# Image keys of eight batches as four pairs with seven products instead of eight

## What is computed

```
q     = heads(x @ to_q_w)
h_txt = sdpa(q, heads(ctx[0:77]   @ to_k_w),        heads(ctx[0:77]   @ to_v_w))
h_obj = sdpa(q, heads(ctx[77:81]  @ to_k_object_w), heads(ctx[77:81]  @ to_v_object_w))
h_oth = sdpa(q, heads(ctx[81:85]  @ to_k_others_w), heads(ctx[81:85]  @ to_v_others_w))
h_ip  = sdpa(q, heads(ctx[85:512] @ to_k_ip_w),     heads(ctx[85:512] @ to_v_ip_w))
out   = merge(h_txt + h_obj + h_oth + h_ip) @ to_out_w + to_out_b + x
```

## Time and profile before

| | |
|---|---|
| median of three runs | 2381.95 us |
| the profiled execution | 2381.67 us, its span 2379.5 us |
| TensorE busy | 2365.9 us |
| VectorE busy | 1835.2 us |
| ScalarE busy | 1775.6 us |
| GpSimd busy | 412.5 us |
| image-key products, line 1661 | 1848 matmuls, 364.2 us |
| granted TensorE clock | 1.00 |
| moved by transfers | 370.12 MB, 156 GB/s in the mean |

### The profile page before, as it was taken

One profiled execution on the slowest core, in us unless ns is written; L12 is line 12 of the kernel. 1 busy time (PEld: TensorE's weight loads), 2 busy tenths in 40 slices (PEclk: granted clock), 3 DMA queues, 4 the chain that ended last, 5 costly groups with the idle time before them and its releaser, 6 DMA issues.

```text
span 2379.5 us, 37663 instructions
## 1 busy us (share of the span) xinstructions
PE 2365.9 (99%) x12801; PEld 1805.1 (76%) x12801; DVE 1835.2 (77%) x3291; ACT 1775.6 (75%) x3906; POOL 412.5 (17%) x564
## 2 busy tenths in 40 slices
PE   9999999999999999999999999999999999999999
PEld 8999999998999986566666666666666666666665
DVE  4457777732333489999999999999999999999994
ACT  4343433332223369999999999999999999999995
POOL 0000000000000023413223133133132231231310
PEclk9999999999999999999999999999999999999999
DMA  9445444374644555545555555555455555555542
GB/s 339 161 128 159 150 136 141 109 268 147 232 167 174 182 174 153 148 129 154 152 143 146 134 148 159 137 146 151 128 156 154 134 150 141 144 161 128 147 132 78
DMA packets 371749, 370.12 MB, mean 156 GB/s; under 512 B 110046, under 2 KB 298590, under 8 KB 371558
## 3 DMA queue, kind: packets, MB, share of 16 engines
q1 hardware_dynamic: 334384, 306.14, 46.7%
q10 hardware_dynamic: 37174, 61.59, 7.0%
HBM read 215.57 MB, written 83.89 MB: 126 GB/s over the span
## 4 chain that ended last, share of the span: by engine, by line
PE 97%; ACT 2%; issue 0%; DMA 0%; DVE 0%; ACTq 0%
PE st_ps L1661 17%; PE s_ps L489 13%; PE st_ps L509 12%; PE om_ps L523 12%; PE om_ps L544 11%; PE om_ps L567 11%; PE s_ps L1713 7%; PE om_ps L1713 4%; PE s_ps L1681 3%; PE st_ps L1713 3%; ACT s_ps L689 1%; PE om_ps L1730 1%; ACT probs L681 1%; PE om_ps L602 1%; PE st_ps L1621 0%
## 5 line engine op out<-in xcount | busy, mean ns | idle before, releaser
L689 ACT ACTIVATE s_ps<-s_ps,negmax 128x427 f32<-128x427 f32 x1280 | 767.8, 608 | 21.6 <-DVE small L759 21.6
L750 DVE TENSOR_REDUCE negmax<-s_ps 128x2 f32<-128x854 f32 x640 | 666.0, 1041 | 75.4 <-PE s_ps L489 69.1
L681 ACT ACTIVATE probs<-st_ps 128x1024 f32<-128x1024 f32 x632 | 656.1, 1038 | 15.2 <-PE st_ps L509 3.7
L489 PE MATMUL s_ps<-kpack,qpack 96*128 96x512 f32 x1280 | 420.9, 410 | 2.1 <-ACT s_ps L689 2.1
L509 PE MATMUL st_ps<-qpack,kpack 104*128 104x512 f32 x1264 | 405.4, 402 | 2.5 <-ACT probs L681 2.5
L447 POOL TENSOR_TENSOR small<-small,negmax 128x616 f32<-128x616 f32 x160 | 196.5, 1228 | 999.8 <-DVE negmax L767 999.6
L1661 PE MATMUL st_ps<-ctx_split,w_split_ip 128*128 128x428 f32 x1848 | 364.2, 358 | 0.0
L1661 PEld LDWEIGHTS st_ps<-ctx_split,w_split_ip 128*128 128x128 f32 x1848 | 347.4, 188 | 15.2 <-issue 1.0
L489 PEld LDWEIGHTS s_ps<-kpack,qpack 96*128 96x128 f32 x1280 | 223.4, 189 | 177.6 <-ACT s_ps L689 81.0
L544 PE MATMUL om_ps<-xs,wq 128*128 128x512 f32 x1200 | 340.6, 394 | 0.0
L567 PE MATMUL om_ps<-heads,wo 128*128 128x512 f32 x1125 | 320.8, 394 | 0.0
(11 more groups left out here) (116 smaller groups left out, 2437.8 us busy)
## 6 DMA issues: line engine op xcount, KB each, us to landing
qpack<-q_out SPq DMA_DIRECT2D x240, 256.0 KB, 4.7
kpack<-kT SPq DMA_DIRECT2D x240, 217.5 KB, 2.9
kT<-k_out ACTq DMA_DIRECT2D x154, 217.5 KB, 3.3
ctx_split_raw<-in_ctxT SPq DMA_DIRECT2D x128, 214.0 KB, 4.6
tok_pair<-in_ctxT SPq DMA_DIRECT2D x48, 512.0 KB, 4.7
xs_raw<-in_xT SPq DMA_DIRECT2D x85, 256.0 KB, 3.8
out<-in_xT SPq DMA_DIRECT2D x75, 256.0 KB, 4.0
out_yT<-out SPq DMA_DIRECT2D x75, 256.0 KB, 2.1
```

The source lines that it names most:

```text
L489: last = nc.tensor.matmul(s_ps[:, n % 2, z, :], qpack[r][0:ROWS_S, j, t * P:(t + 1) * P], kpack[r][0:ROWS_S, j, :], start=True, stop=True)
L681: nc.scalar.activation(probs[:, at:at + 2, :], transposed(u, duo), ACT.Exp).then_inc(p_done, 1)
L689: last = nc.scalar.activation(s_ps[:, n % 2, z, SMALL:TOK], s_ps[:, n % 2, z, SMALL:TOK], ACT.Exp, bias=negmax[:, r, IP, j, t:t + 1], accu ...
L750: nc.vector.tensor_reduce(negmax[:, r, IP, j, t0:t0 + 2], s_ps[:, n % 2, :, SMALL:TOK], AX_X, ALU.max, negate=True).then_inc(s_max, 1)
```

## The change

The batches 3 to 10 are taken in four pairs. In a pair, B11 and B21 are the two halves (512 channels each) of the first batch's context, B12 and B22 those of the second's; the weights of the output blocks 0 and 1 and of 2 and 3 form the other operand, in the same halves. T1 to T4 are sums of the context halves, S1 to S4 sums of the weight halves. Seven products of halves then give the eight that the four double blocks need, with additions at the end. The fifth block is made for each batch as before, in two halves.

A pair is 18 groups (`K_GROUPS`: number of the operand, kind of bank, half), each 4 chunks times three passes, 12 matmuls. The eight operands of a pair (`K_OPERANDS`: B11, T3, T2, T4, B21, T1, B22, B12) go through three slots (`K_SLOTS`), each split in one piece of 4 x 428 elements. VectorE makes the sums T (`key_sum`) and the additions (`add_group`); an addition stands ahead of the split of the same step. ScalarE copies the first product (`keep_x`) and ten blocks per pair (`keep_group`). The stores of a pair's blocks are issued by SP (`store_group`), which also loads the raw context of the pair after next behind the store of group 14 (`load_raw`). The weight sums S are loaded, summed and split in batch 2. The small products move up by one batch each, and the loads of `wq` and `x` move behind all pairs.

```diff
+K_PAIRS = ((3, 4), (5, 6), (7, 8), (9, 10))
+K_PAIRED = tuple(b for pair in K_PAIRS for b in pair)
+K_OPERANDS = (B11, T3, T2, T4, B21, T1, B22, "B12")
+K_SLOTS = 3
+K_GROUPS = ((0, "X", 0), (0, "X", 1), (0, "F", 0), (1, "Q", 0), (1, "Q", 1), (2, "U", 0), (2, "U", 1),
+            (3, "Q", 0), (3, "Q", 1), (4, "X", 0), (4, "X", 1), (4, "F", 0), (5, "U", 0), (5, "U", 1),
+            (6, "U", 0), (6, "U", 1), (6, "F", 1), (7, "F", 1))
+K_OUT = {7: (0, 2), 8: (0, 3), 9: (0, 0), 10: (0, 1), 11: (0, 4), 12: (1, 2), 13: (1, 3), 14: (1, 0), 15: (1, 1), 17: (1, 4)}
+K_OUT_ORDER = tuple(K_OUT.values())
+U_ADDS = 10
+S_PARTS = (S1, S2, S3, S4)
...
-        ORDER += [("k", run, m) for m in k_slots(run)]
-        ORDER += {TXT + 1: [("s", 2, 0)], TXT + 2: [("s", 3, 0)]}.get(run, [])
+        if run - TXT not in K_PAIRED:
+            ORDER += [("k", run, m) for m in k_slots(run)]
+        elif K_PAIRED.index(run - TXT) % 2 == 0:
+            ORDER += [("p", K_PAIRED.index(run - TXT) // 2, i) for i in range(len(K_GROUPS))]
+        ORDER += {TXT: [("s", 2, 0)], TXT + 1: [("s", 3, 0)]}.get(run, [])
...
+    SUMS[("k", before_pairs, 0)] = ("sw", 0)
+    for m, parts in ((1, (S3, S2)), (2, (S1, S4))):
+        SPLITS.setdefault(("k", before_pairs, m), []).extend(("sw", i, 0) for i in parts)
+    for pp in range(len(K_PAIRS)):
+        ahead = [("k", before_pairs, 3), ("k", before_pairs, 4)] if pp == 0 else [("p", pp - 1, 15), ("p", pp - 1, 17)]
+        for j, step in enumerate(ahead + [("p", pp, i) for i in (2 if pp else 0, 3, 6, 9, 11, 13)]):
+            SPLITS.setdefault(step, []).append(("z", pp, j))
+    T_SUMS = {}
+    for pp in range(len(K_PAIRS)):
+        ahead = [("k", before_pairs, 3), ("k", before_pairs, 4)] if pp == 0 else [("p", pp - 1, 16), ("p", pp, 0)]
+        for i, step in zip((T3, T2, T4, T1), ahead + [("p", pp, 3), ("p", pp, 7)]):
+            T_SUMS[step] = (i, pp)
...
+    def stage_done(engine, z):
+        pp, j = divmod(z, len(K_OPERANDS))
+        if j in (0, 1, 6):
+            engine.wait_ge(z_acc, 3 * pp + {0: 1, 1: 2, 6: 3}[j])
+        elif j == 2:
+            engine.wait_ge(u_acc, 4 * pp + 4)
+        else:
+            engine.wait_ge(k_acc, pair_base(pp) + {3: 2, 4: 5, 5: 7, 7: 10}[j])
...
+        def store_group(pp, i):
+            run, m = pair_block(pp, i)
+            k0 = k_num(run, m)
+            sp.wait_ge(k_lo, k0 + 1)
+            sp.wait_ge(k_fill, k0 - k_base(TXT) + 1)
+            for part in (HI, LO):
+                sp.dma_start(d["kT"][run - TXT, part, m * P:(m + 1) * P, N_TXT:TOK],
+                             k_out[:, k0 % KR, part, 0:SM + IPN - 1].bitcast(F32)).then_inc(k_stored[k0 % KR], 16)
+        def load_raw(pp):
+            if pp < 2:
+                sp.wait_ge(k_acc, k_base(before_pairs + pp))
+            else:
+                sp.wait_ge(piece_lo, split_upto(("z", pp - 2, len(K_OPERANDS) - 1)))
+            for h, k in ((0, 0), (1, 1), (1, 0), (0, 1)):
+                sp.dma_start(raw[pp % 2][:, h, k, :, :],
+                             d["ctxT"][K_PAIRS[pp][h], k * CC2 * P:(k + 1) * CC2 * P, TOK - IPN:TOK]
+                             .rearrange("(n p) t -> p n t", p=P)).then_inc(raw_in[pp % 2][h][k], 16)
...
+        for r in range(2):
+            sp.wait_ge(v_stored[r], 16 * len(range(r, v_all, 2)) + 32 * len(range(r, TILE_PAIRS, 2)))
+        load_s_quarters()
+        load_raw(0)
+        load_raw(1)
+        store_late_small()
+        for pp in range(len(K_PAIRS)):
+            for i in K_OUT:
+                store_group(pp, i)
+                if i == 14:
+                    if pp + 2 < len(K_PAIRS):
+                        load_raw(pp + 2)
+                    else:
+                        for n in range(CC):
+                            load_c(K_LOAD[behind_pairs + pp + 2 - len(K_PAIRS)], n)
+        for b in range(K_PAIRED[-1] + 2, BATCH - 1):
+            if TXT + b > behind_pairs + 1:
                 for n in range(CC):
-                    load_halves("v", 1, n)
-            if b == 4:
-                store_late_small()
-            if b == 5:
+                    load_c(K_LOAD[TXT + b], n)
...
+            elif kind == "z":
+                i, z = K_OPERANDS[n], z_number(which, n)
+                if z < K_SLOTS:
+                    act.wait_ge(s_acc, 4)
+                    act.wait_ge(sv_stored, 32)
+                else:
+                    stage_done(act, z - K_SLOTS)
+                if i in T_ORDER:
+                    act.wait_ge(t_raw, summed(i, which))
+                else:
+                    h, k = {B11: (0, 0), B21: (0, 1), B22: (1, 1), "B12": (1, 0)}[i]
+                    act.wait_ge(raw_in[which % 2][h][k], raw_landed(which))
+                nc.scalar.activation(slots[z % K_SLOTS][:, HI, :, :], z_raw(which, n), ACT.Copy).then_inc(piece_hi, 1)
...
+        def keep_x(pp, t):
+            act.wait_ge(u_acc, 4 * pp + t + 1)
+            if pp > 0:
+                act.wait_ge(u_add, U_ADDS * pp)
+            nc.scalar.activation(u2_k[:, t, :], bank(pp, "X", t), ACT.Copy).then_inc(x_sb, 1)
+        def keep_group(pp, i):
+            run, m = pair_block(pp, i)
+            k0, (to, at, n) = k_num(run, m), k_cols(run)
+            _, kind, t = K_GROUPS[i]
+            if kind in "QU":
+                act.wait_ge(u_add, U_ADDS * pp + {7: 5, 8: 6, 12: 7, 13: 8, 14: 9, 15: 10}[i])
+            else:
+                act.wait_ge(k_acc, k0 + 1)
+            act.wait_ge(k_stored[k0 % KR], stored_upto(k0 % KR, k0))
+            src = u3_k[:, t, :] if i in (12, 13) else bank(pp, kind, t)
+            nc.scalar.activation(k_out[:, k0 % KR, HI, to:to + n], src[:, at:at + n], ACT.Copy).then_inc(k_hi, 1)
...
+        def key_sum(i, pp):
+            b11, b21, b12, b22 = (raw[pp % 2][:, h, k, :, :] for h in range(2) for k in range(2))
+            if i == T3:
+                if pp == 0:
+                    dve.wait_ge(s_acc, 4)
+                    dve.wait_ge(sv_stored, 32)
+                else:
+                    dve.wait_ge(piece_lo, split_upto(("z", pp - 1, 1)))
+                dve.wait_ge(raw_in[pp % 2][1][1], raw_landed(pp))
+                dve.wait_ge(raw_in[pp % 2][1][0], raw_landed(pp))
+                to, a, b, op = t3_raw[:, :, :], b22, b12, ALU.subtract
+            elif i == T2:
+                if pp > 0:
+                    dve.wait_ge(piece_lo, split_upto(("z", pp - 1, 2)))
+                dve.wait_ge(t_raw, summed(T3, pp))
+                dve.wait_ge(raw_in[pp % 2][0][0], raw_landed(pp))
+                to, a, b, op = t2_raw[:, :, :], t3_raw[:, :, :], b11, ALU.add
+            elif i == T4:
+                stage_done(dve, z_number(pp, 3) - K_SLOTS)
+                dve.wait_ge(t_raw, summed(T2, pp))
+                dve.wait_ge(raw_in[pp % 2][0][1], raw_landed(pp))
+                to, a, b, op = z_raw(pp, 3), b21, t2_raw[:, :, :], ALU.subtract
+            else:
+                stage_done(dve, z_number(pp, 5) - K_SLOTS)
+                to, a, b, op = z_raw(pp, 5), b12, b11, ALU.subtract
+            nc.vector.tensor_tensor(to, a, b, op).then_inc(t_raw, 1)
...
+        def add_group(pp, i):
+            _, kind, t = K_GROUPS[i]
+            u2, u3, n = u2_k[:, t, :], u3_k[:, t, :], U_ADDS * pp
+            if i in (5, 6):
+                dve.wait_ge(u_acc, 4 * pp + t + 3)
+                dve.wait_ge(x_sb, 2 * pp + t + 1)
+                if pp > 0:
+                    dve.wait_ge(u_add, n)
+                    dve.wait_ge(k_lo, pair_base(pp) - 3)
+                nc.vector.tensor_tensor(u2, bank(pp, "U", t), u2, ALU.add).then_inc(u_add, 1)
+                dve.wait_ge(u_add, n + 2 * t + 1)
+                nc.vector.tensor_tensor(u3, bank(pp, "Q", t), u2, ALU.add).then_inc(u_add, 1)
+            elif i in (7, 8, 14, 15):
+                k0 = k_num(*pair_block(pp, i))
+                dve.wait_ge(k_acc, k0 + 1)
+                dve.wait_ge(u_add, n + (4 if i < 10 else 8))
+                nc.vector.tensor_tensor(bank(pp, kind, t), bank(pp, kind, t), u2, ALU.add).then_inc(u_add, 1)
+            elif i in (12, 13):
+                dve.wait_ge(k_acc, k_num(*pair_block(pp, i)) + 1)
+                dve.wait_ge(u_add, n + 4)
+                nc.vector.tensor_tensor(u3, bank(pp, kind, t), u3, ALU.add).then_inc(u_add, 1)
+        def keep_group(pp, i):
+            run, m = pair_block(pp, i)
+            k0, (to, at, n) = k_num(run, m), k_cols(run)
+            _, kind, t = K_GROUPS[i]
+            src = u3_k[:, t, :] if i in (12, 13) else bank(pp, kind, t)
+            dve.wait_ge(k_hi, k0 + 1)
+            nc.vector.tensor_tensor(k_out[:, k0 % KR, LO, to:to + n], src[:, at:at + n],
+                                    k_out[:, k0 % KR, HI, to:to + n].bitcast(F32), ALU.subtract).then_inc(k_lo, 1)
...
+            if kind == "p":
+                add_group(a, b)
+                if b - 1 in K_OUT:
+                    keep_group(a, b - 1)
+                if b == len(K_GROUPS) - 1:
```

(117 more changed lines are left out.)

54 lines of the change are left out of this document (46 added, 8 removed).

## The result

The changed kernel takes 2368.57 us in the median (2368.26 to 2369.55, four runs), the kernel before 2382.11 us (2381.77 to 2382.32, four runs) on the same chip: the ratio is 0.9942, with an interval of [0.993, 0.9954]. That is 13.5 us less; 2367.7 us were forecast. The profiled execution took 2368.36 us, span 2366.6.

A forecast was written before the change was run, and what follows sets the result against it. TensorE was taken as the bound, busy 2365.9 of 2379.5 us. 2381.7 - 18.7 (matmuls) + 4.6 (transitions) = 2367.6, against the median 2367.9; forecast 2367.7 us, 8-in-10 range 2362.5 to 2376.5.

The forecast's parts named there:

- What the change takes away: Key stage: a pair needs 216 matmuls where two batches cost 240, at 0.1952 us each; four pairs save 18.7 us.
- The four durations: Lengths taken from earlier trace rows for VectorE's long and short operations and ScalarE's splits and copies: 1.94, 0.60, 1.62, 0.53 us.
- L: A VectorE sum or lower split of 1712 elements: 1.94 us, ends 1.49 and 2.28.
- H: ScalarE's upper split of 1712 elements: 1.62 us, ends 1.26 and 1.90.
- The transition: Between two pairs: a 22.1 us VectorE and ScalarE chain makes TensorE wait 1.3 us before group 7; three times, 4.6 us lost.
- The first pair and the edges: The first pair's operands are made beside batch 2, batch 11's splits in groups 14 to 17; claimed loss 0.
- Transfers, 0: Moved loads arrive in time and stores on SP, at 4.2 us landing, keep no place of k_out waiting; claimed loss 0.
- Stores leave ScalarE: In the pairs' blocks, stores move off ScalarE, which loses 0.81 us of issuing per block, none on the path.
- No wait at all: Rival, at the transitions: the chain is 1.3 us shorter, so TensorE never waits; 2363.0 us, chance 0.12.
- VectorE as the bound: Rival, in the pairs: longer VectorE operations or a wrongly walked order of waits; between 2371 and 2377 us, chance 0.17.
- The ring: Rival: late stores on SP hold up k_out's four places, then ScalarE, VectorE and TensorE; slower than before, 2389 or 2409 us, chance 0.06.

## Why the prediction was right

- **What the change takes away.** 888 matmuls at line 1940 and 864 at line 1987 are the 1752 that were forecast; a pair without a wait lasts 42.18 us, where two batches took 46.8. Four times that is 18.5 us (forecast 18.7).
- **The four durations.** The rows of the trace after, by form, answer to the earlier trace rows (busy us, mean ns, idle ahead):

```profile
L1687 DVE TENSOR_TENSOR k_ops<-ctx_raw,k_ops 128x1712 fp32r<-128x1712 f32 x16 | 31.0, 1935 | 3.1 <-ACT k_ops L1484 3.1
...
L1484 ACT ACTIVATE k_ops<-t_raw 128x1712 fp32r<-128x1712 f32 x8 | 13.1, 1635 | 19.3 <-DVE t_raw L1727 18.3 <-POOL k_out L1875 1.0
...
L1759 DVE TENSOR_TENSOR om_ps<-om_ps,u_k 128x428 f32<-128x428 f32 x8 | 4.8, 605 | 2.1 <-PE om_ps L1987 2.1
```

  L was 1.94 in the prediction, H 1.62, the addition written back into PSUM 0.60 of 0.60 to 0.68: all three were right within 1%. The straight line between two sizes held.
- **The transition.** Forecast 22.1 us for the chain, 1.3 us of wait, 1.5 us with the weight load, three times 4.6 in all; measured 22.20, 1.28 to 1.30, 1.5 and 4.6. T2 was 0.7 us early for group 5, as forecast (621.76 against 622.48 us); T3 1.6 us early for group 3 (616.21 against 617.79), where 0.7 was forecast. The prediction's own durations give 1.4 there (10.3 us of chain, group 3 due 11.7 us after group 15); its 0.7 was a slip on which nothing else rests.
- **The first pair and the edges** cost nothing: PE's waits show none there.
- **Transfers, 0.** No copy of the pairs waited for a store. The stores of 568 to 742 us landed in 2.5 us (median), where 4.2 was taken. But SP's one queue does what was feared. Its timeline in the first pair's last groups:

```profile
608.25 2.53 SPq L1342 DMA_DIRECT2D ctx_raw<-in_ctxT  x4
610.88 4.32 SPq L1332 DMA_DIRECT2D kT<-k_out  x4
```

  The stores issued from 604 to 606.5 us, ahead of these loads, and the four from 609 to 616 us, behind them (count, KB each, median us to landing):

```profile
kT<-k_out SPq DMA_DIRECT2D x2, 217.5 KB, 2.1
...
kT<-k_out SPq DMA_DIRECT2D x4, 217.5 KB, 8.5
```

  A store behind the 3424 KB takes 8.5 us in the median (10.3 the first) instead of 2.1, and as its place is wanted only some 25 us later, nobody waits. That is what the Trainium skill's "DMA: Bandwidth & Descriptors" (Queues, rings and completion order) says of one ring worked off in order; the trace agrees. With three places one copy of the pairs waited for a store (1.6 us), and TensorE for none.
- **Where it was wrong: "Stores leave ScalarE, which loses 0.81 us of issuing per block, none of it on the path."** True of the kernel before, where that sentence came from, but not of the changed one: with the stores left on ScalarE the change gains nothing (2381.39 us). With this order of the sums the move is not a detail beside the change but a condition of it, and the forecast came out because it was made in the same diff. With T2 behind T3 it is no condition: there most of the gain is left with the stores on ScalarE (2371.4 us).
- **The rivals.** No wait at all (2363.0) is what the version with T2 moved comes to, 2364.11. VectorE as the bound: with 130 us of work in 173 it wasn't. The ring: not in the pairs.
- **What stays open.** The last key block starts 13.94 us earlier (872.29 and 858.35 us), near the 14.1 forecast; the end of the span only 12.9. From that block's start to the end there are 1507.21 us in the trace of before, 1508.25 after, and between 1507.4 and 1508.3 in the experiments. So up to 1 us is lost in attention, as large as the spread between these traces; no run here tells what it is.

## What to carry to other kernels

When TensorE is the bound, work moved onto half-idle engines is free only if their order is: walk the list of each in-order engine through the one place where operands are made one behind another, with durations taken from rows of nearby sizes, and compare its length with what TensorE still has to do. Where a sum is split by one engine and finished by another, put the next sum between, so that the two engines work on different operands. What looks free on an engine with slack (an issue, a store) must be looked at again at that place.
